# Block attention and a mixture of experts on one core: six batches routed as one group, two computed with all experts, with new orders of the engines

## The reference

```python
x = x + attention(layernorm(x), Wq, Wk, Wv, Wo)
x = x + experts(layernorm(x), router_gate, expert_gate_up, expert_down)
# attention: scores per block of 32 keys, softmax WITHIN each block; the blocks up to the query's own
# are added and divided by their number; inside the query's own block later keys are masked
# experts: logits = h @ router_gate.T; top 2 of softmax, their scores made to sum to 1
#   expert e: (up * silu(gate)) @ expert_down[e], gate and up the even and odd columns of h @ expert_gate_up[e]
```

## Time and profile before

| what | us |
|---|---|
| median of 3 runs | 395.83 (390.98 to 397.88) |
| profiled execution: its own time | 389.57 |
| profiled execution: span of its instructions | 387.8 |
| mean granted TensorE clock | 0.976 of full |

### The profile page before, as it was taken

The page is one execution under the profiler, slowest core; times in us unless marked ns, Lnnn a source line. Parts: engine busy times, 40 slices in busy tenths (PEclk is TensorE's granted clock), DMA queues, the critical chain, the costliest instruction groups (busy, mean ns, idle before and its releaser), DMA issues.

```text
span 387.8 us, 9335 instructions
## 1 busy us (share of the span) xinstructions
PE 343.4 (89%) x2888; PEld 309.9 (80%) x2888; DVE 246.4 (64%) x708; ACT 173.4 (45%) x428; POOL 220.0 (57%) x477
## 2 busy tenths in 40 slices
PE   0677888899998998999989996999998999989984
PEld 0666767799997997998988996998887898868863
DVE  3424866345799856769857579666685343376677
ACT  3553161545533445453452562345654556546200
POOL 8533555575765886765786766551362221787350
PEclk9988999999999999999998999699999999999999
DMA  7479974769772319277157014113466424666441
GB/s 234 79 178 232 242 166 89 227 194 159 200 155 67 124 57 153 52 122 166 43 112 161 2 42 165 42 54 103 125 212 218 132 88 123 183 196 212 146 122 54
DMA packets 45955, 52.66 MB, mean 136 GB/s; under 512 B 5012, under 2 KB 38932, under 8 KB 45716
## 3 DMA queue, kind: packets, MB, share of 16 engines
q1 hardware_dynamic: 43220, 44.73, 46.4%
q0 software_dynamic: 2688, 7.34, 6.2%
HBM read 30.56 MB, written 21.50 MB: 134 GB/s over the span
## 4 chain that ended last, share of the span: by engine, by line
PE 62%; POOL 14%; DVE 12%; issue 7%; ACT 3%; DMA 1%; DVEq 0%; POOLq 0%; ACTq 0%
PE bank L1074 15%; PE bank L971 10%; PE bank L1149 9%; PE bank L1161 4%; PE bank L1043 3%; PE bank L1120 3%; POOL xs_d L719 3%; PE bank L1061 2%; DVE nmax L773 2%; PE bank L1012 2%; PE bank L1140 2%; POOL fold L685 2%; DMA raw<-ys_d,back_i 1%; PE bank L1046 1%; ACT VB L574 1%
## 5 line engine op out<-in xcount | busy, mean ns | idle before, releaser
L1074 PE MATMUL bank<-VB,PT 128*128 128x68 f32 x768 | 97.1, 278 | 1.2 <-ACT PT L587 0.8
L1074 PEld LDWEIGHTS bank<-VB,PT 128*128 128x128 f32 x768 | 92.4, 195 | 2.2 <-ACT PT L587 2.0
L587 ACT ACTIVATE PT<-bank 128x384 f32<-128x384 f32 x128 | 57.0, 494 | 62.1 <-PE bank L1064 61.9
L773 DVE TENSOR_REDUCE nmax<-bank 128x12 f32<-128x384 f32 x128 | 63.9, 552 | 9.2 <-PE bank L1046 8.5
L685 POOL TENSOR_TENSOR fold<-oblk 128x128 f32<-128x128 f32 x64 | 29.1, 455 | 42.1 <-DVE oblk L783 37.2
L1149 PE MATMUL bank<-wgu_sb,xgt 128*128 x168 | 45.3, 395 | 1.8 <-ACT y_sb L617 1.7
L780 DVE RECIPROCAL linv<-bank 128x24 f32<-128x24 f32 x64 | 19.6, 306 | 37.5 <-PE bank L1074 37.2
L783 DVE TENSOR_TENSOR oblk<-bank,linv 128x384 f32<-128x384 f32 x64 | 35.7, 558 | 9.9 <-POOL o_sb L694 8.0
L1043 PE MATMUL bank<-KS,QS 96*128 96x256 bf16 x128 | 36.6, 286 | 5.8 <-ACT VB L574 2.4
L1061 PE MATMUL bank<-QS,KS 120*128 120x256 bf16 x128 | 36.0, 281 | 5.3 <-DVE nmax L773 4.1
L733 POOL DMA_INDIRECT raw<-ys_d,back_i x28 | 27.2, 971 | 17.1 <-issue 7.2
(11 more groups left out here) (156 smaller groups left out, 847.6 us busy)
## 6 DMA issues: line engine op xcount, KB each, us to landing
parts_d<-parts SPq DMA_DIRECT2D x16, 384.0 KB, 3.3
KS<-parts_d SPq DMA_DIRECT2D x42, 128.0 KB, 4.9
xg<-xs_d SPq DMA_DIRECT2D x42, 128.0 KB, 2.1
ys_d<-y_sb SPq DMA_DIRECT2D x42, 128.0 KB
QS<-parts_d SPq DMA_DIRECT2D x7, 384.0 KB, 7.1
xs_d<-zeros SPq DMA_DIRECT2D x18, 128.0 KB, 2.2
...
```

The costliest lines, as they stand in the source:

```text
L587: nc.scalar.activation(PT[u % NPT][:, k % 2, :], bank[BANK["B", b, k]][:, 0:SC], ACT.Exp, scale=SCALE)\
L773: nc.vector.tensor_reduce(nmax[b % 2][:, 0:NC_, k], bank[BANK["A", b, k]][:, 0:SC] .rearrange("p (c s) -> p c s", s=BS), AX.X, ALU.max, ne ...
L1074: last = pe.matmul(o[:, at:at + PW], PT[u % NPT][:, n, src:src + P], v[:, t, 2 * k + n, :], start=True, stop=True)
```

## The change

1. `GROUPS` is one group of batches 0 to 5 (31 tiles), and `DENSE` are batches 6 and 7. The dense units get a running number over both batches (`dense_number`), which all their waits count by. The dense temporaries move from PT to `rest` and `xn[0]`, and the turned x2 of batch 7 has a place of its own in `xn[1]`, that of batch 6 stays in x2t. `weight` has a copy per dense batch. cu, ad, rw, sc, gb and cb of batch 6 and tab1, ga1 are gone.
2. GpSimd clears the value buffers later: z0 behind ln0, z1 behind ln2.
3. SP stores and loads K's stacks of batches 0 to 2 ahead of Q's where Q's came first; stores of the parts go in the same order on GpSimd.
4. TensorE runs twelve products of the identity with itself (`WARM`) into bank 7 when the constants have come, before its first unit.
5. All five orders are new from end to end.

Core of the diff; of the orders only the places that are spoken of:

```diff
+WARM = 12
...
-GROUPS = ((0, 1, 2, 3, 4), (5, 6))
+GROUPS = ((0, 1, 2, 3, 4, 5),)
-DENSE = 7
+DENSE = (6, 7)
...
 SP_ORDER
-    "xl0 cst0 wl0.0-1 tabs0 xl1 xl2 xl3 blk0 wl0.2 qP0 kP0 stq0.0-1 stk0.0-1 qP1 kP1 xl4 xl5 xl6 xl7 stq1 stk1 "
-    "qP2 kP2 mS0 stq2 stk2 mL0 qP3 mS1 kP3 we0.0 mL1 we0.1 qP4 we0.2 kP4 we0.3-6 stk3 stq3 we0.7-11 stk4 stq4 qP5 "
...
+    "xl0 cst0 wl0.0-1 tabs0 xl1 xl2 xl3 blk0 wl0.2 kP0 qP0 stk0.0-1 stq0.0-1 kP1 xl4 xl5 xl6 xl7 qP1 stk1 stq1 "
+    "mS0 kP2 qP2 mL0 stk2 stq2 we0.0-1 kP3 we0.2-4 qP3 we0.5 stk3 we0.6 stq3 we0.7 mS1 mL1 kP4 mS2 qP4 we0.8 mL2 "
...
 POOL_ORDER
-    "zz0 z0 z1 ln0 ln1 ln2 ln3 qP0 kP0 qP1 kP1 qP2 kP2 ms0 ln4 ln5 ln6 ln7 ms1 qP3 kP3 os0.0 qP4 os0.1 kP4 "
...
-    "ms7 mb5 rw5 sc5.0-3 rw6 sc6.0-3 os7.0-5 gb0.0-1 os7.6 gb0.2-3 gb1.0-2 os7.7 gb1.3 gb2.0-3 gb3.0 res7 gb3.1-3 "
-    "gb4.0-3 gb5.0-3 gb6.0-3"
+    "zz0 ln0 z0 ln1 ln2 z1 kP0 qP0 ln3 kP1 qP1 ms0 kP2 qP2 ln4 ln5 ln6 ln7 ms1 kP3 os0.0-2 qP3 os0.3-7 ms2 kP4 "
...
+    "sc3.3 os5.3-7 mb4 rw4 sc4.0 ms6 sc4.1 res5 sc4.2-3 ms7 rw5 sc5.0-3 os6.0-7 res6 os7.0-7 res7 gb0.0-3 gb1.0-3 "
+    "gb2.0-3 gb3.0-3 gb4.0-3 gb5.0-3"
 DVE_ORDER
-    "o5.2-6 am7.0-2 o5.7 top4 am7.3-4 ad4 oS5 tab0 o6.0 ga0 o6.1-2 am7.5-6 sr4 res5 o6.3 am7.7-8 o6.4-7 ta0.0-1 "
...
-    "ta1.12-13 top7 ta1.14 cb3 da7.0 sr7 da7.1 we7 cb4 da7.2 dc7.0 da7.3 dc7.1 cb5 da7.4 dc7.2 da7.5 dc7.3 cb6 "
-    "da7.6 dc7.4 da7.7 dc7.5-7"
+    "ln0 w0.0-1 xS0 ln1 ln2 ln3 qS0 kS0 xS1 w0.2 kS1 qS1 xS2 am0.0-15 kS2 xS3 qS2 ln4 ln5 ln6 ln7 am1.0-15 kS3 "
...
+    "res4 ad3 sr3 o5.0 am6.7-8 o5.1 am6.9 o5.2-6 am6.10-11 o5.7 am6.12-14 top4 oS5 ad4 sr4 am6.15 res5 am7.0-15 "
+    "top5 ad5 tab0 sr5 ga0 o6.0-5 ta0.0-2 o6.6 ta0.3-4 o6.7 ta0.5-6 oS6 ta0.7 res6 ta0.8-10 o7.0 ta0.11-12 o7.1 "
...
+    "top6 ta0.27 sr6 res7 we6 ta0.28 da6.0 ta0.29 da6.1 ta0.30 da6.2-3 dc6.0-1 top7 da6.4 sr7 da6.5 we7 dc6.2 cb0 "
+    "da6.6-7 dc6.3-4 cb1 dc6.5 da7.0-1 dc6.6-7 cb2 da7.2-3 dc7.0-1 cb3 da7.4-5 dc7.2-3 cb4 da7.6 dc7.4 da7.7 cb5 "
+    "dc7.5-7"
 PE_ORDER
+    "A1.0@5 A1.1@3 A1.2@2 A1.3@5 A1.4@3 A1.5@2 xT4@7 A1.6@5 A1.7@3 A1.8@2 A1.9@5 A1.10@3 A1.11@2 A1.12@5 A1.13@3 "
+    "A1.14@2 A1.15@5 B0.0@3 B0.1@2 B0.2@5 B0.3@3 PV0.0@2 B0.4@7 B0.5@3 PV0.1@4 B0.6@3 B0.7@2 PV0.2@7 B0.8@2 "
...
+    "mT6@0 A7.5@1 A7.6@2 A7.7@7 A7.8@1 A7.9@2 A7.10@7 A7.11@1 A7.12@2 x2T5@0 A7.13@7 A7.14@1 A7.15@2 rt5@0 B6.0@2 "
+    "B6.1@1 B6.2@7 cu5@0 B6.3@2 PV6.0@1 B6.4@2 B6.5@0 PV6.1@7 B6.6@0 B6.7@2 PV6.2@4 tr0.0 tr0.1 tr0.2 tr0.3 tr0.4 "
+    "tr0.5 B6.8@7 B6.9@1 PV6.3@2 B6.10@1 B6.11@4 PV6.4@7 B6.12@4 B6.13@2 tx0.0@1 PV6.5@0 tg0.0@1 tx0.1@2 tx0.2@7 "
...
-    "dg7.2@5 dg7.3@3 dg7.4@2 dd7.0@1 dg7.5@5 dd7.1@1 dg7.6@3 dd7.2@1 dd7.3@2 dg7.7@1 dd7.4@5 dd7.5@2 dd7.6@3 "
-    "dd7.7@1"
+    "td0.24@6 tx0.29@1 tT0.26@2 wo7@5 tg0.28@2 td0.25@0 tx0.30@4 tT0.27@1 dg6.0@6 tg0.29@5 td0.26@2 td0.27@1 "
+    "tT0.28@6 dg6.1@4 tg0.30@2 td0.28@1 tT0.29@6 dg6.2@5 tT0.30@6 td0.29@2 dg6.3@1 td0.30@2 dd6.0@6 dd6.1@2 "
+    "x2T7@4 dg6.4@5 rt7@6 dg6.5@2 dd6.2@4 dd6.3@1 dg6.6@5 dd6.4@6 dg6.7@2 dd6.5@4 dg7.0@5 dg7.1@2 dd6.6@6 dd6.7@1 "
+    "dg7.2@5 dg7.3@2 dd7.0@1 dd7.1@6 dg7.4@5 dg7.5@2 dd7.2@6 dd7.3@1 dg7.6@5 dg7.7@2 dd7.4@1 dd7.5@6 dd7.6@5 "
+    "dd7.7@2"
...
+def dense_number(b, k):
+    return NE * DENSE.index(b) + k
...
-        dth, dgs, dhid = ([PT[n][:, :, :].rearrange("p a s -> p (a s)")[:, S * a:S * (a + 1)] for n in range(2)]
-                          for a in range(3))
+        dth, dgs, dhid = ([w[:, :, :].rearrange("p a s -> p (a s)")[:, S * n:S * (n + 1)] for n in range(2)]
+                          for w in (rest[0], rest[1], xn[0]))
+        x2t_d = [x2t[:, :, :], xn[1][:, :, :]]
...
+            for n in range(WARM):
+                pe.matmul(bank[7][:, 0:P], ident_f, ident_f, start=True, stop=True)
...
                 if stage == "dg":
                     if k == 0:
...
                     for a in range(2):
                         for kt in range(KT):
-                            last = pe.matmul(dst[:, S * a:S * (a + 1)], wgu_sb[:, k, kt, NI * a:NI * (a + 1)], x2t[:, kt, :],
+                            last = pe.matmul(dst[:, S * a:S * (a + 1)], wgu_sb[:, k, kt, NI * a:NI * (a + 1)], x2_turned(b)[:, kt, :],
```

More of the change, by code:

```diff
@@ L224, in group_of @@
     return next((g for g, members in enumerate(GROUPS) if b in members), None)
-COUNTED = [len([n for n in range(b) if n != GROUPS[group_of(n)][-1]]) for b in range(NB)]
+COUNTED = [len([n for n in range(b) if group_of(n) is not None and n != GROUPS[group_of(n)][-1]]) for b in range(NB)]
 NTABSTEP = 16
@@ L349, in preln_block_attention_moe @@
         y_sb = [sb(f"y_sb{n}", [P, H], F32) for n in range(NY)]
-        dth, dgs, dhid = ([PT[n][:, :, :].rearrange("p a s -> p (a s)")[:, S * a:S * (a + 1)] for n in range(2)]
-                          for a in range(3))
+        dth, dgs, dhid = ([w[:, :, :].rearrange("p a s -> p (a s)")[:, S * n:S * (n + 1)] for n in range(2)]
+                          for w in (rest[0], rest[1], xn[0]))
+        x2t_d = [x2t[:, :, :], xn[1][:, :, :]]
         share = sb("share", [P, TOP, TT, NE], F32)
-        weight = sb("weight", [P, TT, NE], F32)
+        weight = sb("weight", [P, len(DENSE), TT, NE], F32)
         bank = [pb(f"bank{n}") for n in range(8)]
@@ L416, in half, with x2_turned @@
             return bank[t][:, :].rearrange("p (k s) -> p k s", k=KT)
+        def x2_turned(b):
+            return x2t_d[DENSE.index(b)] if b in DENSE else x2t[:, :, :]
         @block.sync
@@ L515, in _ @@
                 if stage == "dx":
-                    if b == DENSE:
-                        sp.wait_ge(added, TT * NE)
+                    if b in DENSE:
+                        sp.wait_ge(added, TT * dense_number(b, NE))
                     else:
@@ L557, in _ @@
                     wait(act, ready["rt"], b)
-                    nc.scalar.copy(x2t[:, :, :], half(BANK["x2T", b, 0])).then_inc(drained["x2T"], 1)
+                    nc.scalar.copy(x2_turned(b), half(BANK["x2T", b, 0])).then_inc(drained["x2T"], 1)
                 if stage in ("qS", "kS"):
@@ L592, in _ @@
                 if stage == "dt":
-                    act.wait_ge(ready["dg"], k + 1)
-                    wait(act, dgs_done, k - 1)
-                    nc.scalar.activation(dth[k % 2], bank[BANK["dg", b, k]][:, 0:S], ACT.Tanh, scale=0.5).then_inc(dtanh_done, 1)
+                    n = dense_number(b, k)
+                    act.wait_ge(ready["dg"], n + 1)
+                    wait(act, dgs_done, n - 1)
+                    nc.scalar.activation(dth[n % 2], bank[BANK["dg", b, k]][:, 0:S], ACT.Tanh, scale=0.5).then_inc(dtanh_done, 1)
                 if stage == "tS":
@@ L914, in _ @@
                 if stage == "we":
+                    n = DENSE.index(b)
                     dve.wait_ge(score_step, 5 * (b + 1))
+                    wait(dve, weight_step, 2 * n)
                     nc.vector.tensor_tensor(share[:, :, :, :], is_rank[:, b, :, :, :],
                                             score[:, b, :, :].unsqueeze(3).to_broadcast([P, TOP, TT, NE]), ALU.mult).then_inc(weight_step, 1)
-                    dve.wait_ge(weight_step, 1)
-                    nc.vector.tensor_tensor(weight[:, :, :], share[:, 0, :, :], share[:, 1, :, :], ALU.add).then_inc(weight_step, 1)
@@ L920, in _ @@
-                    dve.wait_ge(weight_step, 2)
+                    dve.wait_ge(weight_step, 2 * n + 1)
+                    nc.vector.tensor_tensor(weight[:, n, :, :], share[:, 0, :, :], share[:, 1, :, :], ALU.add).then_inc(weight_step, 1)
+                    dve.wait_ge(weight_step, 2 * n + 2)
                 if stage == "da":
+                    n = dense_number(b, k)
                     src = bank[BANK["dg", b, k]]
-                    dve.wait_ge(dtanh_done, k + 1)
-                    wait(dve, drained["dg"], k - 1)
@@ L925, in _ @@
-                    nc.vector.scalar_tensor_tensor(out=dgs[k % 2], in0=dth[k % 2], scalar=1.0, in1=src[:, 0:S],
+                    dve.wait_ge(dtanh_done, n + 1)
+                    wait(dve, drained["dg"], n - 1)
+                    nc.vector.scalar_tensor_tensor(out=dgs[n % 2], in0=dth[n % 2], scalar=1.0, in1=src[:, 0:S],
                                                    op0=ALU.add, op1=ALU.mult).then_inc(dgs_done, 1)
-                    dve.wait_ge(dgs_done, k + 1)
-                    wait(dve, ready["dd"], k - 1)
@@ L929, in _ @@
-                    nc.vector.scalar_tensor_tensor(out=dhid[k % 2], in0=src[:, S:2 * S], scalar=0.5, in1=dgs[k % 2],
+                    dve.wait_ge(dgs_done, n + 1)
+                    wait(dve, ready["dd"], n - 1)
+                    nc.vector.scalar_tensor_tensor(out=dhid[n % 2], in0=src[:, S:2 * S], scalar=0.5, in1=dgs[n % 2],
                                                    op0=ALU.mult, op1=ALU.mult).then_inc(drained["dg"], 1)
                 if stage == "dc":
-                    dve.wait_ge(ready["dd"], k + 1)
+                    n = dense_number(b, k)
@@ L933, in _ @@
```

(19 more changed lines are left out.)

## The result

The changed kernel took 396.6 us in the median of 20 runs (393.17 to 408.11), the kernel before 396.36 in the same session. The ratio is **1.0097, 95% interval 1.0055 to 1.0138**: some 4 us slower, where 2.3 us faster was forecast. The median lies inside the forecast's 384 to 402 us, but the change went the other way. The profiled execution took 394.6 us (span 392.7), 5.0 more than that of before. Some executions of both kernels have a spell of 25 to 40 us at the lower TensorE clock in the middle of the attention: the medians hold them, the ratios leave them out, and of the profiled executions that have one (e4_fill, e14_more, e15_beforefill) only rows outside it are read.

What follows compares the result with a forecast made beforehand. TensorE, busy 343.4 of 387.8 us, was taken as the bound, time being lost where it stands. Start -3.9, tiles -19.4 and -1.4, tables +6.4, end +16.0 sum to -2.3 on the median of 395.83: 393.5 us, range 384 to 402.

Steps and rivals of the forecast that it cites:

- the start: Up to the first B: later buffer clearing and K before Q bring B0.0 near 57, partly moved work; -3.9 us.
- the table stretch: Where the tables are made: TensorE stands and then loses clock, 13.7 us against 7.3 now; +6.4 us.
- the end: Last routed product to the end: dense units and gathers nearly balance three engines, 41.3 us against 25.3; +16.0 us.
- the tiles: Tile phase: eleven tiles fewer, more dense first products before the last routed product, -19.4; tab1 and ga1 leave, -1.4 us.
- the first A at about 34: Start: with K loaded before Q, the first scores of batch 0 come 1.5 us earlier.
- at 0.50 us each: end at 42: Start: batch 0's 16 VectorE reductions run without others between them and end at 42 (now 45.8).
- not before 62: Start: sign that the term is wrong, if B0.0, forecast near 57, does not come before 62 us.
- under the 7 that I had named as refuting it: Tables: the term is wrong if TensorE's idle time in the 28 us before B6.8 is under 7 us.
- the same loss at the low level, 3 us: Tables: after B6.8's wait of about 4 us for o6.1, TensorE loses 3 us at its lower clock.
- stands 10.7 us: Tables: TensorE has 17.1 us of work during VectorE's 27.8 us in one piece, so it stands 10.7 us.
- The rival that ended faster: Whole kernel: orders fit as laid out, table stretch costs 0, start gives 5, tiles go at 2.0; 385 us, chance 0.26.
- the slower one: End: hand-over bounds the dense units at a pitch of 3.45 us each; +17.7 us, 411 us, chance 0.11.

Runs made afterwards that it cites:

- e4_fill: Changed kernel with extra, unused TensorE products ahead of A7.0 to A7.10, cu5 and B6.8; 393.31 us, ratio 1.0069.
- e14_more: Changed kernel with edits of e10_fill_b68 and e11_start, plus extra products ahead of A0.0 and q3; 384.95 us, ratio 0.9888.
- e15_beforefill: Kernel before with register loads one at a time and sixteen extra products ahead of B6.8; 390.67 us, ratio 1.0011.
- e11_start: Experiment 10: changed kernel with z1 behind ln3 and one of q2, k2, v2 behind every three A; 394.16 us, ratio 1.0089.
- Experiments 3: Changed kernel with the clearing z1 behind ln3 instead of ahead of kP0; 395.42 us, ratio 1.0133.
- 9: Changed kernel with q2 and k2 behind A0.0 to A0.2 and z1 behind ln3; 394.59 us, ratio 1.0083.
- 12: Same run as e14_more: changed kernel with e10_fill_b68, e11_start and extra products ahead of A0.0 and q3; 384.95 us, ratio 0.9888.
- e10_fill_b68: Experiment 7: changed kernel with register loads one at a time and extra products ahead of A7.0 to A7.10, cu5 and B6.8; 389.14 us, ratio 0.9958.

## Why the prediction was wrong, step by step

The sum of -2.3 us became +4.9 in the profiled execution. Of the 7.2 us between them the start has 3.1, the table stretch 1.3, the end 2.8; the tiles were right.

**Start: the step that failed most.** The steps on GpSimd came as put: first statistics step at 4.96, K's parts at 20.8. The forecast then took "the first A at about 34" from the loads, and its reductions "at 0.50 us each: end at 42". Missed were words of TensorE's new order: q2 and k2 between v1 and A0.0, v2 behind A0.2 (the kernel before has the three behind A0.2, A0.5 and A0.8, much as e11_start has), and q3 ahead of mT0. The first A came at 36.48, 2.5 us late. The reductions ran from 36.97 to 45.5, 3.5 late, with 0.86 of waiting at v2. The split of the maxima was done at 48.1, but mT0 stood behind q3, at half speed, until 49.50, where "near 45" was forecast:

```profile
46.80 0.55 PE L979 MATMUL bank<-xt_h,wqkv_h 128*128 128x256 f32 x1 [2.22 <-DVE xt_l L765]
...
49.50 0.70 PE L1062 MATMUL bank<-tables_b,mpart 128*128 128x128 bf16 x6
...
53.46 7.53 DVE L777 TENSOR_REDUCE nmax<-bank 128x12 f32<-128x384 f32 x16 [2.33 <-PE bank L1056]
```

The first reduction of batch 1 waited 2.33 us for TensorE, where the forecast had VectorE go straight on, and the sixteen of them set the pace to the first B at 60.11, 3.1 us late; the sign of being wrong, "not before 62", was not met. Experiments 3, 9 and 10 show that the loads and the clearing were not the limit, and 12 that the clock, once q2, k2 and v2 stood between the A, was worth 2.1 us of the first B.

**Tables: the sum nearly right, the mechanism not.** Forecast were 10.7 us of standing and 3 at the low level. In the 28 us before B6.8 TensorE stood 4.9 (23.09 busy of 28.00), under the 7 that I had named as refuting it, and B6.8 (251.78) waited for nothing. VectorE's piece was counted well: it ran from 219.99 to 250.73, 28.2 us of work against 27.8, and 2.5 of waits. TensorE was so slow beside it (at the lower level from 224 to 234 and from 240.9 on) that it reached B6.8 only 1.05 us behind the end of o6.1, and VectorE was no longer felt. VectorE's line of o6.1 is the fourth:

```profile
230.44 0.40 PE L1053 MATMUL bank<-KS,QS 96*128 96x256 bf16 x1 [2.02 <-DVE nmax L777]
...
241.17 0.17 PE L1112 MATMUL bank<-chosen,tables_b 128*128 128x16 bf16 x1 [1.39 <-issue]
...
241.84 2.77 PE L1084 MATMUL bank<-VB,PT 128*128 128x68 f32 x12
...
250.17 0.56 DVE L787 TENSOR_TENSOR oblk<-bank,linv 128x384 f32<-128x384 f32 x1
...
251.78 0.37 PE L1071 MATMUL bank<-QS,KS 120*128 120x256 bf16 x1
...
256.43 2.77 PE L1084 MATMUL bank<-VB,PT 128*128 128x68 f32 x12
...
262.95 2.01 PE L1159 MATMUL bank<-wgu_sb,xgt 128*128 x4
```

The term that was mis-sized is "the same loss at the low level, 3 us": 23.9 us at 0.50 are 12 us of lost work. Only what lies behind the end of o6.1 is lost to the whole. From B6.8 to the first product of a tile TensorE took 11.2 us (251.78 to 262.95), and 5.9 in e10_fill_b68 (250.91 to 256.84), at full speed with B6.8 released by VectorE. With that, filling the stands gave about 6 us back (the last routed product at 342.4 instead of 348.6, experiment 7). The term "stands 10.7 us" failed the other way: the work at half speed filled most of it. That the two errors nearly cancelled in the sum (+7.7 against +6.4) is luck. The rival that ended faster priced the stretch at 0 and the slower one did not name it; no rival had the clock as its mechanism, though the price of a unit at the low level was in my rows.

The Trainium skill, page "TensorE: Matmul & The Clock Gate", Part 1, says that the clock is low by default and that activity releases it. What WARM did agrees with both (0.28 instead of 0.42 us for a product of q0 behind it). From 240.9 on the second does not hold as it stands: 23.63 us of work in 23.90 did not release the clock, and the measurement decides.

**Tiles: right.** -20.9 against -20.8: eleven tiles, two more dense first products, x2T7 and rt7 behind, tab1 and ga1 gone. The forecast price of 1.9 a tile held.

**End: right in kind, two terms too small.** The forecast had 35.9 us of VectorE's work, 2.8 of stops and 2.6 of store. In the trace the last dc ends 41.6 us behind the last routed product: 38.0 of work, 3.6 of stops (the longest 1.2 for a second product, 0.70 for rt7, 0.68 for raw at cb5), and 2.5 of store. The mis-sized term is the addition to the output: the sixteen dc took 14.4 us, 0.90 each, instead of 12.5 at 0.78. The 0.78 was one dc with another unit behind it; here most follow one another, and two take 1.76 to 1.95. Beside the thirteen pairs of activations half of a fourteenth lay there, and the stops were 0.8 longer, 1.9 of them ahead of top7 (2.2 forecast), 1.8 elsewhere (0.6). VectorE's last rows:

```profile
370.72 0.88 DVE L964 SCALAR_TENSOR_TENSOR raw<-raw,score,x_all 128x256 f32<-128x256 f32 x2 [0.29 <-DMA raw<-ys_d,back_i]
...
385.79 0.88 DVE L964 SCALAR_TENSOR_TENSOR raw<-raw,score,x_all 128x256 f32<-128x256 f32 x2 [0.68 <-DMA raw<-ys_d,back_i]
...
387.38 2.83 DVE L945 SCALAR_TENSOR_TENSOR x_all<-bank,weight,x_all 128x256 f32<-128x256 f32 x6
```

The gathers came 1.25 us apart with a few at 1.5. The dense units had a pitch of (378.52 - 373.24) / 2 = 2.64 us against 2.4 to 2.6, and the slower rival's 3.45 did not come. VectorE was 82% busy (36.27 of 44.10) and not over 90: the gaps between its short instructions count as idle, which my sum by pitches had included.

**WARM, no cost and no gain:** right.
